# A four-layer decoder on one core: the last attention batch runs into the MLP, the first MLP runs into the next cross attention, and cross keys and values are projected from split operands

## The reference, cut to what matters

```python
# layer 0: causal self attention, cross attention to the context, MLP (256 -> 1024 -> 256)
x = x + attend(ln(x)) ; x = x + cross(ln(x), ctx) ; x = x + mlp(ln(x))
# layer 1: cross attention whose weights are quantized first
gamma = mean(|W|) ; Wq = W + (clip(round(W / (gamma + 1e-5)), -1, 1) * gamma - W)
x = x + cross(ln(x), ctx; Wq)
# layer 2: masked self attention, cross attention, MLP ; layer 3: causal attention of wide heads
```

## Time and profile before

| | us |
|---|---|
| median of 3 runs | 3936.55 |
| the profiled execution's own time | 3936.01 |
| its span | 3934.2 |
| PE busy | 3657.2 (93%) |
| DVE busy | 2777.7 (71%) |
| ACT busy | 2459.2 (63%) |
| POOL busy | 1989.8 (51%) |
| TensorE clock granted, mean | 0.955 of full |

### The profile page before, as it was taken

One profiled execution on the slowest core, in us unless ns is written; L12 is line 12 of the kernel. 1 busy time (PEld: TensorE's weight loads), 2 busy tenths in 40 slices (PEclk: granted clock), 3 DMA queues, 4 the chain that ended last, 5 costly groups with the idle time before them and its releaser, 6 DMA issues. The chain is left out here.

```text
span 3934.2 us, 68606 instructions
## 1 busy us (share of the span) xinstructions
PE 3657.2 (93%) x21586; PEld 2042.0 (52%) x21586; DVE 2777.7 (71%) x6843; ACT 2459.2 (63%) x5254; POOL 1989.8 (51%) x1987
## 2 busy tenths in 40 slices
PE   6999999997996999999999999998799999999998
PEld 3444444443882344433333334443687777777776
DVE  4666677774665777788999978774766666666664
ACT  2555567775331677778888877776325666666665
POOL 3555533322322323358888843231445677776765
PEclk7999999998996999989999899999899999999999
DMA  4433353431002434333222244431100000000000
GB/s 106 100 85 82 80 113 84 86 84 48 1 1 49 116 88 89 78 67 86 62 63 63 60 99 89 89 83 49 45 1 12 12 7 12 13 7 12 12 1 12
DMA packets 135373, 220.51 MB, mean 56 GB/s; under 512 B 42720, under 2 KB 44640, under 8 KB 133216
## 3 DMA queue, kind: packets, MB, share of 16 engines
q1 hardware_dynamic: 135008, 216.02, 23.7%
HBM read 59.69 MB, written 5.51 MB: 17 GB/s over the span
## 5 line engine op out<-in xcount | busy, mean ns | idle before, releaser
L1105 ACT ACTIVATE prob<-ST 128x512 f32<-128x512 f32 (+3 forms) x2304 | 1151.3, 567 | 440.0 <-PE ST L647 435.9
L1343 DVE TENSOR_REDUCE mx<-MX 128x1 f32<-128x512 f32 x1536 | 964.2, 683 | 221.7 <-PE MX L647 220.2
L647 PE MATMUL MX<-stk 48*128 48x512 f32 (+3 forms) x2560 | 897.5, 441 | 59.2 <-DVE mx L1336 14.3
L647 PE MATMUL ST<-stk 50*128 50x512 f32 (+3 forms) x2560 | 917.8, 444 | 2.6 <-ACT prob L1105 1.8
L647 PEld LDWEIGHTS MX<-stk 48*128 48x128 f32 x2560 | 420.6, 191 | 707.1 <-DVE mx L1343 293.6
L1788 POOL TENSOR_SCALAR prob<-prob,mx 128x128 f32<-128x128 f32 (+3 forms) x512 | 558.5, 1104 | 274.1 <-DVE mx L1523 274.1
L647 PE MATMUL OUT<-prob,V 128*32 128x512 f32 (+3 forms) x5120 | 664.4, 592 | 8.0 <-POOL prob L1730 4.1
L647 PEld LDWEIGHTS ST<-stk 50*128 50x128 f32 x2560 | 424.3, 189 | 51.1 <-ACT prob L1105 23.8
L1336 DVE CUSTOM_DVE_ANT_0 MX<-MX,W_even 128x512 f32<-128x512 f32 x512 | 348.0, 701 | 39.3 <-PE MX L647 38.7
L1723 POOL TENSOR_TENSOR prob<-prob,W_odd 128x512 f32<-128x512 f32 x256 | 324.8, 1283 | 90.7 <-ACT prob L1105 90.3
L1340 DVE CUSTOM_DVE_ANT_0 MX<-MX,later 128x128 f32<-128x128 f32 (+3 forms) x512 | 238.0, 519 | 124.8 <-PE MX L647 124.0
(11 more groups left out here) (190 smaller groups left out, 7254.8 us busy)
## 6 DMA issues: line engine op xcount, KB each, us to landing
stk<-hi SPq DMA_DIRECT2D x640, 128.0 KB, 3.8
stk<-lo SPq DMA_DIRECT2D x320, 128.0 KB, 3.9
misc<-misc SPq DMA_DIRECT2D x160, 128.0 KB, 2.6
sums<-spread SPq DMA_DIRECT2D x80, 256.0 KB
misc<-in_ctx_t SPq DMA_DIRECT2D x24, 512.0 KB, 6.8
W_even<-in_w SPq DMA_DIRECT2D x2, 2048.0 KB, 10.1
XH<-in_ctx_rows SPq DMA_DIRECT2D x8, 512.0 KB, 3.5
X<-in_x_t SPq DMA_DIRECT2D x1, 3584.0 KB, 14.0
```

Source lines behind the costliest of these rows:

```text
L647: return nc.tensor.matmul(o, l, r, start=start, stop=stop)
L1105: nc.scalar.activation(prob_at(k)[:, q0:S], STB[k % RING][:, q0:S], ACT.Copy if addmask else ACT.Exp).then_inc(ex_done, 2 if addmask else 1)
L1343: nc.vector.tensor_reduce(m, bank[:, :], AX.X, ALU.max).then_inc(mx_red, 1)
```

## The change

- Cross keys and values: the context (a cast and a subtraction on POOL, `ctx_parts`) and the K and V weights (`keys_values_parts`, or ACT and DVE for CROSS1) are split into high and low fp32r parts, and each fp32 product becomes three one-pass products, high by high, low by high and high by low.
- Attention to MLP (both MLPs): batch 0 of the MLP is normed in slot 13, turned in slot 15 in places K0 and K1, batch 1 is normed in slot 16. The stops at `x_done` go. The weight split waits for the last value product only, and the last batch's output projection is done in the MLP's first batch, after f = 3 and f = 4.
- MLP0 to CROSS1: the quantization is cut into seven steps that DVE does in the MLP's batches 1 to 6. Batch 0 of CROSS1 is normed and turned in the MLP's last batch. CROSS1 begins with the Q of its first unit.

```diff
--- before.py
+++ after.py
-        ctxT = misc[:, 0:4, :].rearrange("p (a c) n -> p a c n", a=2)
-        ones = XH[:, 0, 0:P]
+        ones = sums[:, 0, 0:P]
+        q_up = nc.alloc_sbuf_tensor_at("q_up", [P, 4, 512], F32, offset=hot)
+        ctx_hi = nc.alloc_sbuf_tensor_at("ctx_hi", [P, 2, NC, S], F32R, offset=misc_at)
+        ctx_lo = nc.alloc_sbuf_tensor_at("ctx_lo", [P, 2, NC, S], F32R, offset=pr_at + 4 * 1024)
+        ctx_full = nc.alloc_sbuf_tensor_at("ctx_full", [P, 2, NC, S], F32, offset=pr_at + 4 * 1024)
+        kv_hi = nc.alloc_sbuf_tensor_at("kv_hi", [P, 2, NC, E], F32R, offset=pr_at + 4 * 3072)
+        kv_full = W[1][:, 512:1536].rearrange("p (m c o) -> p m c o", m=2, c=NC)
...
+        def to_mlp(s, u, at=UNITS):
+            return s + 1 in MLP_NO and u == at
         def norm_of(s, u):
+            if to_mlp(s, u, UNITS - 3):
+                return s + 1, 0
+            return turn_of(s, u)
+        def turned_ahead(s, u):
+            return (s, u) == (CROSS1, -2)
...
                 if cross and s not in JOINED:
-                    load_ctx(0, 0)
                     load_ctx(1, 1)
+                if s == MLP0:
+                    sp.dma_start(ctx1_full[:, :, :], ctx_in[:, 0:NC, :]).then_inc(ctx_in_sem[0], 16)
                 if s == CROSS1:
+                    sp.wait_ge(l_full, L_NO[s, -1, "V1"] + 1)
                     sp.dma_start(mask_q, masks_in[:, 0:NT, :]).then_inc(masks_loaded, 16)
...
+                    if turned_ahead(s, u):
+                        pe.wait_ge(first1_free, 2)
+                        begin(u, "Q")
+                        for cc in range(NC):
+                            project(wq(sa, 0), half, hT, cc)
+                    if turned_ahead(s, u - 1):
+                        pe.wait_ge(pr_evac, 2 * NB)
...
-                                    pe.wait_ge(ctx_in_sem[1 - par], 16 * (4 * CROSS_NO[sa] + pa + 1))
+                                    pe.wait_ge(ctx_low, ctx_no(sa, ba) + 1)
+                                    pe.wait_ge(kv_low, CROSS_NO[sa] + 1)
...
+                            if to_mlp(s, u, UNITS - 1) and r == place[f"K{part}"]:
+                                begin(u, f"F{part}")
+                                transpose_x(s + 1, 0, part, L).then_inc(l_full, 1)
...
+                def project_parts(m, half, source, c):
+                    for n, (a, b) in enumerate(THREE):
+                        last = mm(L[:, :], (kv_hi, kv_lo)[a][:, m, c, P * half:P * half + P], source[b][:, c, :],
+                                  c == 0 and n == 0, c == NC - 1 and n == 2)
...
+                def project_values_parts(source, j, t):
+                    for n, (a, b) in enumerate(THREE):
+                        for c in range(NC):
+                            last = mm(Lt[:, t, :], source[a][:, c, tok], (kv_hi, kv_lo)[b][:, 1, c, :],
+                                      n == 0 and c == 0, n == 2 and c == NC - 1)
...
+                def last_out(j):
+                    if j == 0:
+                        pe.wait_ge(at_ready, BASE + 2 * NB * (ATTN_NO[s - 1] + 1))
+                    pe.wait_ge(l_free, L_NO[s - 1, UNITS, f"O{j}"])
+                    project_out(s - 1, j)
...
+                        if b == 0 and f in (3, 4):
+                            last_out(f - 3)
...
+                    else:
+                        pe.wait_ge(xh_ready, NB * CROSS1 + 1)
+                        pe.wait_ge(ml_evac, turn_no(m, NB))
+                        for c, bank in enumerate((LA, LB)):
+                            turn_tiles(c, bank).then_inc(first1_full, 1)
...
+                    if s + 1 == CROSS1 and b == 1:
...
+                        mm(LA[:, 0:4], ones, qabs[:, :]).then_inc(quant_pe, 1)
-                turn(0)
...
             for s in range(8):
-                if s not in JOINED and s != SELF3:
-                    wait(pe, x_done, NB * s)
-                    pe.wait_ge(w_in[s], 16)
...
+                def first_turned(u, U, c):
+                    act.wait_ge(l_full, L_NO[s, u, f"F{c}"] + 1)
...
+                    nc.scalar.activation(hi[:, c, :], L[:, :], ACT.Identity, **scale_shift(s + 1, c)).then_inc(ml_hi, 1)
+                    nc.scalar.activation(hT[:, c, :], L[:, :], ACT.Identity, **scale_shift(s + 1, c)).then_inc(l_free, 1)
...
                     act.wait_ge(w_in[s], 16)
+                    act.wait_ge(pv_done, 8 * UNITS * (ATTN_NO[s - 1] + 1))
...
-                turned(0)
...
-                if s not in JOINED and s != SELF3:
-                    wait(act, x_done, NB * s)
+                if s == CROSS1:
+                    act.wait_ge(quant, QUANT_STEPS)
+                    act.wait_ge(pr_full, 2 * NB)
+                    nc.scalar.activation(kv_hi[:, :, :, :], kv_full, ACT.Copy).then_inc(kv_high, 1)
...
+                    if to_mlp(s, u):
+                        dve.wait_ge(x_done, NB * s + 2)
+                        layer_norm_x(NB * (s + 1) + 1, 1)
...
+                    if to_mlp(s, u, UNITS - 1):
+                        for c in range(NC):
+                            dve.wait_ge(l_free, L_NO[s, u, f"F{c}"] + 1)
+                            low_normed(c)
...
+                    if first1:
+                        dve.wait_ge(x_done, NB * s + 1)
+                        layer_norm_x(NB * CROSS1, 0)
                     for f in range(NF):
                         split_hidden(b, f)
+                        if s + 1 == CROSS1 and b in (1, 2) and f == 2:
+                            quantize(b - 1)
+                        if b == 0 and f in (3, 4):
+                            output_sum((s - 1, NB - 1), L_NO[s - 1, UNITS, f"O{f - 3}"], f - 3)
...
+                    if s + 1 == CROSS1 and 2 <= b < 7:
+                        quantize(b)
...
-                layer_norm_x(NB * s, 0)
-                weights_low()
-                low_turned(0)
+                weights_low(range(2))
+                invert(UNITS * (ATTN_NO[s - 1] + 1), 1)
+                weights_low(range(2, 8))
...
                 if s == CROSS1:
-                    quantize()
-                    dve.wait_ge(quant, QUANT_STEPS)
-                scale_queries(s, W[s % 2][:, 0:512], HD ** -0.5)
+                    dve.wait_ge(kv_high, CROSS_NO[CROSS1] + 1)
+                    nc.vector.tensor_tensor(kv_lo[:, :, :, :], kv_full, kv_hi[:, :, :, :].bitcast(F32),
+                                            ALU.subtract).then_inc(kv_low, 1)
...
+            def ctx_parts(sc, b):
...
+                pool.wait_ge(ctx_in_sem[par], 16 * (N // 2 + 1))
+                nc.gpsimd.tensor_copy(high, full).then_inc(ctx_high, 1)
+                pool.wait_ge(ctx_high, N + 1)
+                nc.gpsimd.tensor_tensor(low, full, high.bitcast(F32), ALU.subtract).then_inc(ctx_low, 1)
...
+                    if to_mlp(s, u):
+                        layer_norm(NB * (s + 1) + 1, xt(1, 0, NT), l_full, L_NO[s, u - 1, "F1"] + 1)
...
+                    if cross and half == 0 and 0 <= b < NB - 2:
+                        ctx_parts(s, b + 2)
+                    if s + 1 in JOINED and s + 1 in CROSS_NO:
+                        if u in (4, 6):
+                            ctx_parts(s + 1, u // 2 - 2)
+                        if u == 8:
+                            keys_values_parts(s + 1)
...
-                layer_norm(NB * s, xt(0, 0, NT))
...
+                    if s + 1 == CROSS1 and b == 1:
+                        nc.gpsimd.memset(ones, 1.0).then_inc(ones_set, 1)
+                        ctx_parts(CROSS1, 0)
+                    if s + 1 == CROSS1 and b + 1 == NB:
+                        layer_norm(NB * CROSS1, xt(0, 0, NT), ml_full, turn_no(m, NB))
```

More of the change, by code:

```diff
@@ L653, in transpose_x, with project_out @@
                 return turn_tiles(c, bank)
+            def project_out(so, j):
+                for t in range(2):
+                    tok = slice(P * (2 * j + t), P * (2 * j + t) + P)
+                    for k in range(2):
+                        last = mm(Lt[:, t, :], raw[:, k, tok], wq(so, 3)[:, k, :], k == 0, k == 1)
+                last.then_inc(l_full, 1)
             def turn_tiles(c, bank):
@@ L694, in slot @@
                             values(s, U, half, par, VALUES[lag][r])
-                        if half == 0 and on["a"] and r == place["T1"]:
+                        if half == 0 and on["a"] and r == place["T1"] and not turned_ahead(s, u):
                             begin(u, "T1")
@@ L1053, in slot @@
                     sa, _ = a_of(s, u, b)
-                    if u == -2:
+                    if u == -2 and not turned_ahead(s, u):
                         normalized(sa, u, 0)
+                    if turned_ahead(s, u):
+                        high_part(sa, u, U, half, 1)
                     place = AT[addmask]
@@ L1077, in slot @@
                             rows_out(u, U + 1, 0)
-                        if half == 1 and r == place["T0"] and norm_of(s, u) is not None:
-                            normalized(norm_of(s, u)[0], u, 0)
```

(18 more changed lines are left out.)

202 lines of the change are left out of this document (125 added, 77 removed).

## The result

| | before | after |
|---|---|---|
| median, us | 3934.86 (4 runs, 3912.83 to 3937.19) | 3859.22 (4 runs, 3853.86 to 3861.72) |
| ratio | | 0.983, 95% interval 0.981 to 0.9851 |
| profiled execution; its span | 3936.01, 3934.2 | 3861.72, 3860.0 |
| PE busy, instructions | 3657.2, 21586 | 3629.7, 21874 |
| POOL busy | 1989.8 | 2075.9 |

The kernel is faster by about 75 us (1.7%), where 117 were forecast (3.0%): the direction came out, the time lies 1 us outside the range. The two profiled executions differ by 74.3, and that can be split by landmarks that both traces have. The forecast column holds the prediction's own terms, put on the same stretches.

A forecast was written before the change was run, and what follows sets the result against it. PE bounds the cross stages and MLP0, no engine the stops between stages; 24.1 + 23.6 + 30.2 + 44 - 2 - 3 = 116.9 off 3936.0 gives 3819 us, range 3796 to 3858.

The forecast's parts named there:

- Cross keys and values: K and V projections in 24 cross batches: one-pass products save 2.18 us a batch, 1.83 after waits; gain 44, bounds 0 and 52.
- Attention to MLP: Stops at CROSS0 to MLP0 and CROSS2 to MLP2: gains 24.1 and 23.6 us, bounds 20 to 26 each.
- MLP0 to CROSS1: Gap from MLP0's last matmul to CROSS1's first maxima tile: 46.2 us falls to 14.5; gain 30.2 after costs, bounds 26 and 36.
- the three variants that differed in it alone: POOL's product at MLP starts: late 1.5 us (3819, chance 0.47), 3.3 (3823, 0.13), or at most 0.69 (3817, 0.20).
- the lowest: Rival at MLP starts: POOL waits for one DVE instruction only, product late by at most 0.69 us; 3817 us, chance 0.20.
- the row of eight subtractions: First boundary before the change: a four-element POOL instruction took 4.73 us beside DVE's eight subtractions (4.88), read as POOL shut out.
- I take +2: MLP0: quantization moved into DVE's idle time, with POOL's context split, costs 2 us; bounds 0 and 6.
- SELF2: Self stage with less cover for POOL's three context-split blocks of 3.7 us: 1 us lost each, +3, bounds 0 and 11.
- POOL's context split delays the maxima: Rival in the cross stages: late split makes PE wait at M1 in each of 24 batches, up to 3994 us; chance 0.04.
- The projections give nothing: Rival: one-pass K and V in the cross stages save no time, 3819 + 44 = 3863 us; chance 0.10.

The follow-up runs named there:

- the paired kernels: Changed kernel with all four repairs, 16 satisfied waits ahead of SELF3's loop (3811.76 us), and the repairs on fp32 K and V without waits (3829.38 us).
- the kernel with 16 waits: Changed kernel plus MLP0 work and SELF3 weight splitting moved between additions, V's ones set earlier, 16 satisfied waits ahead of SELF3's loop; median 3811.76 us, ratio 0.9716.

## Why the prediction was right and wrong

- **Attention to MLP: right, twice.** 27.9 and 27.8 us came off the gaps, forecast 26.6 and 26.1. POOL's product was late by 0.2 and not 1.5 or 3.3, so of the three variants that differed in it alone the lowest fits. There the rule of the Trainium skill ("SBUF — State Buffer", section "SBUF: two separate sides"), that each of the two holds the port for one whole instruction, describes the trace better than the row of eight subtractions on which I had relied. The rows above agree with it three times in the other direction: DVE's 0.54, 1.23 and 0.42 us instructions took 2.63, 2.98 and 4.83, each until 0.3 to 1.1 us after the end of one instruction of POOL. The row of 4.73 stays an exception to it.
- **MLP0, the step that failed first.** "DVE idles 68 of 194 us, I take +2" treated idle time as one store. The stretch became 21.6 us longer for 3.5: 18 us too few. DVE's idle time lies after the splits and while PE sums; the steps had been put at a batch's end, where DVE's chain (addition, statistics, POOL's norm, the turning) leads straight to PE. The bound of 6 was too low for the same reason. Moved, the same instructions cost what I had said. This is a mistake in the mechanism; the next is one of size.
- **Cross keys and values, the term that was mis-sized.** 44 was forecast; 21 to 23 is what the paired kernels and the stretches give, which makes this the term that missed by most. Of the difference, 24 x 0.92 = 22 comes from the prices. For the old work I took durations with their modelled ends (1.13, 1.99), where start to next start gives 1.06 and 1.93; for the new, a quarter of a run of four (0.27), where the first of a short run takes 0.34 and the part 0.90 in all. The measured 1.26 then loses 0.4 a batch, near the 0.35 that I had counted as waited away. PE's waits for `at_ready` before O0 in CROSS2 rose from 3.2 to 5.4 us and in CROSS0 fell from 3.8 to 3.1.
- **SELF3: not in the sum at all.** The change adds nothing to it, and it took 11 us longer, some 7 of them for the place of its code on PE. No row of before could price it, but it could have been a line of the range.
- **MLP0 to CROSS1: 28.1 for 31.7.** Two steps of 1.8: the low weights held up by POOL's bias addition, which I had running beside them, and DMAs one by one on SP's queue.
- **Why only 43 are missing.** MLP0, the projections, SELF3 and this gap miss by some 56 together. SELF2 and the starts of the two MLPs gave some 10 more than forecast, and the rest is within what single traces differ by. That the time came to within 1 us of the range is in part luck.
- **SELF2 and the end of CROSS2.** SELF2 gained 3.6 where 3 were to be lost; it takes 508.9 to 523.0 in the traces of this study, with either form of K and V (515.9 before, 515.5 in the last kernel), so no sign can be read from it. In CROSS2's last unit the granted clock was 0.78 in the changed kernel (2644 to 2678) and 1.00 in the kernel with 16 waits; 34 us at 0.78 are some 7 of the 14.5 us missing in that stretch. That too comes and goes, and in CROSS0 it made the kernel before the slower one (0.80 against 1.00), so the stretch that matched its forecast of 12.1 did so by luck.
- **The rivals.** "POOL's context split delays the maxima" did not happen: cast and subtraction take 1.04 and 2.37, and PE has no such wait in CROSS0. "The projections give nothing" had nearly the measured time (3863), for another reason: they give 21 to 23, and the rest of the loss is MLP0 and SELF3.

The row of MLP2 stood in the trace of before and I had not looked at it: three batches of 32 us among 24.4 show what a long POOL instruction does to DVE's splits.

## What to carry to other kernels

When work is moved into an engine's idle time, ask which of its gaps it fills: a gap that ends in a wait for the slow engine is free, and the same work ahead of the norm of the next batch costs its whole length plus whatever POOL holds at that moment. Price short runs from start to next start, on both sides of a comparison. When a stage that nobody touched gets slower by the same amount at each pass of a loop, compare the instruction packets of the two pages before looking for a cause in its work.

## What the hardware showed that I had not expected

- 16 more satisfied waits on PE ahead of a loop made every second distance of its batches 3 us shorter (117.0 for about 120) and the stage 4 to 11 (SELF3 958.1 for 962.0 to 969.5), with two instruction packets fewer.
- DVE's cast of 0.42 us took 4.83 beside POOL's 128x2048 subtraction, and a scalar operation of 0.54 took 2.63 beside its bias addition; one on 8 columns still took 2.40, while the norm's statistics beside the same addition kept their 1.40.
- A stop of 2.4 us inside PE's work was followed by 3.7 us at a granted clock of 0.54.
